# Query and key parts as three stored blocks, and the second-pass copies of the first two heads loaded behind the chunk loop

## What is computed

```python
xn = _layernorm(x, axis=-1)                      # x: 2048 tokens of 256
qkv = xn @ qkv_w.T + qkv_b
q, k, v = split(qkv)                             # 16 heads of width 16
scores = einsum('bqhd,bkhd->bhqk', q, k) / sqrt(16)
scores = where(causal, scores + slopes[h] * (pos_k - pos_q), -1e9)
attn = softmax(scores, axis=-1)
out = einsum('bhqk,bkhd->bqhd', attn, v) @ out_w.T + out_b
x = x + out * silu(experts(xn))                  # top 2 of 8 experts for each token
```

## Time and profile before

| what | value |
|---|---|
| runs | 852.41, 852.84, 845.97 us (median 852.41) |
| profiled execution | 851.59 us |
| its span, first to last instruction | 849.8 us |
| PE busy | 714.9 us (84%) |
| DVE busy | 584.8 us (69%) |
| ACT busy | 476.4 us (56%) |
| mean granted TensorE clock | 0.919 of full speed |

### The profile page before, as it was taken

One profiled execution on the slowest core, in us unless ns is written; L12 is line 12 of the kernel. 1 busy time (PEld: TensorE's weight loads), 2 busy tenths in 40 slices (PEclk: granted clock), 3 DMA queues, 4 the chain that ended last, 5 costly groups with the idle time before them and its releaser, 6 DMA issues.

```text
span 849.8 us, 14608 instructions
## 1 busy us (share of the span) xinstructions
PE 714.9 (84%) x5342; PEld 334.9 (39%) x5342; DVE 584.8 (69%) x1190; ACT 476.4 (56%) x990; POOL 156.3 (18%) x297
## 2 busy tenths in 40 slices
PE   3477788668889898998999999989999988888885
PEld 1244364333333444444344434434443442333433
DVE  5999776389667776777677667767776777974121
ACT  2277757450566566566656565656565566645551
POOL 1423250027600000000000100000000006720111
PEclk9688989785799999999999999999999999958998
DMA  9710223435470562253235325422522312330001
GB/s 295 253 35 7 87 90 116 120 96 164 154 134 5 148 127 82 76 128 87 70 105 131 94 72 122 130 70 81 123 87 70 110 70 70 113 118 1 26 26 50
DMA packets 76863, 83.76 MB, mean 99 GB/s; under 512 B 35485, under 2 KB 60512, under 8 KB 76448
## 3 DMA queue, kind: packets, MB, share of 16 engines
q1 hardware_dynamic: 70982, 71.96, 30.5%
q0 software_dynamic: 3280, 8.98, 3.4%
q10 hardware_dynamic: 2530, 1.89, 0.8%
HBM read 39.56 MB, written 25.43 MB: 76 GB/s over the span
## 4 chain that ended last, share of the span: by engine, by line
PE 55%; ACT 13%; DVE 9%; issue 7%; SPq 6%; DMA 4%; POOL 4%; ACTq 2%; POOLq 0%; DVEq 0%
PE bank L1535 15%; PE bank L1472 8%; ACT PR L805 7%; PE bank L1435 7%; PE bank L1445 5%; PE bank L1494 5%; PE bank L1550 4%; SPq L405 4%; PE bank L1307 3%; POOL XT L570 3%; DMA qk_parts<-TG 2%; DVE PM L1206 2%; PE bank L1350 2%; PE bank L1576 2%; ACT U L794 2%
## 5 line engine op out<-in xcount | busy, mean ns | idle before, releaser
L805 ACT ACTIVATE PR<-bank 128x512 f32<-128x512 f32 (+3 forms) x640 | 317.6, 537 | 254.4 <-PE bank L1494 145.3
L1206 DVE TENSOR_REDUCE PM<-bank 128x1 f32<-128x512 f32 (+3 forms) x640 | 354.7, 603 | 75.6 <-PE bank L1472 46.9
L1494 PE MATMUL bank<-OPS 57*128 57x512 f16 (+3 forms) x640 | 210.8, 366 | 54.3 <-ACT PR L805 47.6
L1472 PE MATMUL bank<-OPS 54*128 54x512 f16 (+3 forms) x640 | 197.0, 377 | 12.4 <-DVE PM L1206 8.3
L1535 PE MATMUL bank<-PR,VS 128*17 128x512 f32 (+3 forms) x1280 | 164.1, 565 | 0.0
L1494 PEld LDWEIGHTS bank<-OPS 57*128 57x128 f16 x640 | 53.0, 94 | 119.7 <-ACT PR L805 109.9
L1472 PEld LDWEIGHTS bank<-OPS 54*128 54x128 f16 x640 | 50.0, 95 | 120.3 <-DVE PM L1206 74.2
L538 POOL TENSOR_TENSOR NP<-NM,NIL 128x8 bf16<-128x8 f32 x32 | 7.7, 240 | 464.1 <-DVE NM L1214 463.9
L1435 PE MATMUL bank<-WB 128*128 128x256 f16 x552 | 80.8, 276 | 0.0
L1435 PEld LDWEIGHTS bank<-WB 128*128 128x128 f16 x552 | 46.4, 101 | 35.9 <-issue 29.4
L1504 PE MATMUL bank<-MASK 64*128 64x64 bf16 x512 | 59.6, 199 | 0.0
(11 more groups left out here) (179 smaller groups left out, 783.3 us busy)
## 6 DMA issues: line engine op xcount, KB each, us to landing
WB<-W SPq DMA_DIRECT2D x23, 512.0 KB, 3.8
OPS<-qk_parts SPq DMA_DIRECT2D x56, 128.0 KB
x_rows<-PR SPq DMA_DIRECT2D x23, 256.0 KB, 3.2
WB<-in_w SPq DMA_DIRECT2D x23, 256.0 KB, 3.5
y_rows<-XT SPq DMA_DIRECT2D x23, 256.0 KB, 3.1
OPS<-qk_parts SPq DMA_DIRECT2D x56, 64.0 KB
W<-in_w SPq DMA_DIRECT2D x6, 512.0 KB, 6.0
XT<-in_b SPq DMA_DIRECT2D x23, 128.0 KB, 4.0
```

Source lines behind the costliest of these rows:

```text
L805: act.activation(PR[:, tile % RING, off:CH], PS[2 + tile % 2][:, off:CH], ACT.Exp, scale=1 / SCORE).then_inc(b_exped, 1)
L1206: dve.tensor_reduce(PM[:, c % 2, j, xq, gg:gg + 1], bank[:, 0:width], AX.X, ALU.max).then_inc(a_reduced, 1)
L1472: last = mm(bank[:, 0:width], OPS[ROWS_A, slot, 0, P * (TC * a + xq):P * (TC * a + xq) + P], OPS[ROWS_A, slot, 1, CH * gg:CH * gg + width] ...
L1494: last = mm(bank[:, off:CH], OPS[ROWS_B, slot, 1, P * k:P * k + P], OPS[ROWS_B, slot, 0, CH * b + off:CH * b + CH], start=True, stop=k < T ...
```

## The change

The DRAM tensor qk_parts has three blocks a side instead of two, in the order in which OPS wants them: high, low, high for the queries, high, high, low for the keys. Each of the four staging buffers is therefore stored by two DMAs instead of one (STORES: first part, number of parts, block to write), 8 stores a chunk and 1.5 times the bytes. In return one load fills the 48 rows of one side of a row half (load_parts), and load(h) has 6 DMAs instead of 10.

The loads of heads 0 and 1 are divided. The position rows of row half 0 are loaded once, over all columns, ahead of the chunk loop (rows_in), behind three new waits for phi_q, scan_kv and numden, that the first layer is done with the memory of OPS. In the chunk loop only row half 0 is loaded, 4 loads a chunk. Row half 1 of both heads is loaded behind the loop and behind the UNITS loads, over all columns, with 6 loads (second_in), and the first tile of the second pass waits for it too. All counts of parts_out, first_in and opa_in follow.

```diff
--- before.py
+++ after.py
@@ -32,8 +32,8 @@
 POS = 6
 
 
-LOADS = (((0, 2, 1), (0, 1, 1)), ((0, 1, 2), (1, 1, 1)))
-HEAD_DMAS = 2 * (1 + len(LOADS[0]) + len(LOADS[1]))
+STORES = (((0, 2, 0), (0, 1, 2)), ((0, 1, 0), (0, 2, 1)))
+PART_DMAS = 2
 HALF_ROWS = P // 2
 ROWS = POS + 3 * HD
 ROWS_A = slice(0, ROWS)
@@ -240,7 +240,7 @@
         PROWS = [w2flat[0:ROWS8, 2 * WQG + 1024 * n:2 * WQG + 1024 * n + 1024].bitcast(F16) for n in range(2)]
 
 
-        parts = nc.dram_tensor("qk_parts", (2, 2, D, S), F16, kind="Internal").ap()
+        parts = nc.dram_tensor("qk_parts", (2, 3, D, S), F16, kind="Internal").ap()
         bias_rows = nc.dram_tensor("bias_rows", (3, 3 * D + E), BF16, kind="Internal").ap()
         all_rows = nc.dram_tensor("position_rows", (2, ROWS8, 2, S), F16, kind="Internal").ap()
         x_rows = nc.dram_tensor("x_rows", (SLOTS * BLOCKS, 2 * D), F16, kind="Internal").ap()
@@ -307,7 +307,7 @@
         parts_out = [sem(f"parts_out{m}") for m in range(4)]
         raw_in = [sem("raw_in0"), sem("raw_in1")]
         last_in = [sem("last_in0"), sem("last_in1")]
-        ones_in = sem("ones_in")
+        ones_in, rows_in, second_in = sem("ones_in"), sem("rows_in"), sem("second_in")
         mrow = [sem(f"mrow{s}") for s in range(NC)]
         x_in = [sem(f"x_in{c}") for c in range(NC)]
 
@@ -371,42 +371,32 @@
                 sp.wait_ge(x1_add, 2 * c + 2)
                 sp.dma_start(x1_dram[:, TC * c:TC * c + TC, :], XO[:, TC * c:TC * c + TC, :]).then_inc(x1_spill, 16)
 
+            def load_rows(h, half, done):
+
+                base = HALF_ROWS * half
+                sp.dma_start(OPS[base:base + POS, h % 4, :, :],
+                             all_rows[h // 8, POS * (h % 8):POS * (h % 8) + POS, :, :]).then_inc(done, 16)
+
+            def load_parts(h, half, cols, done):
+
+                base = HALF_ROWS * half
+                for side in range(2):
+                    sp.dma_start(OPS[base + POS:base + ROWS, h % 4, side, cols],
+                                 parts[side, :, HD * h:HD * h + HD, cols]).then_inc(done, 16)
+
             def load(h):
 
-                for base in (0, HALF_ROWS):
-                    sp.dma_start(OPS[base:base + POS, h % 4, :, :],
-                                 all_rows[h // 8, POS * (h % 8):POS * (h % 8) + POS, :, :]).then_inc(opa_in[h // 2 % 2], 16)
-                    for side in range(2):
-                        row = base + POS
-                        for first, parts_of, times_of in LOADS[side]:
-                            rows = HD * parts_of * times_of
-                            src = parts[side, first:first + parts_of, HD * h:HD * h + HD, :]
-                            if times_of > 1:
-                                src = src.broadcast_to([times_of, HD, S])
-                            sp.dma_start(OPS[row:row + rows, h % 4, side, :], src).then_inc(opa_in[h // 2 % 2], 16)
-                            row += rows
-
-            def first_load(c):
-
-                cols = slice(CH * c, CH * c + CH)
-                sp.wait_ge(parts_out[0], 16 * c + 16)
-                sp.wait_ge(parts_out[2], 16 * c + 16)
-                for base in (0, HALF_ROWS):
-                    for h in range(2):
-                        sp.dma_start(OPS[base:base + POS, h, :, cols],
-                                     all_rows[0, POS * h:POS * h + POS, :, cols]).then_inc(first_in[c], 16)
-                        for side in range(2):
-                            row = base + POS
-                            for first, parts_of, times_of in LOADS[side]:
-                                rows = HD * parts_of * times_of
-                                src = parts[side, first:first + parts_of, HD * h:HD * h + HD, cols]
-                                if times_of > 1:
-                                    src = src.broadcast_to([times_of, HD, CH])
-                                sp.dma_start(OPS[row:row + rows, h, side, cols], src).then_inc(first_in[c], 16)
-                                row += rows
+                for half in range(2):
+                    load_rows(h, half, opa_in[h // 2 % 2])
+                    load_parts(h, half, slice(0, S), opa_in[h // 2 % 2])
 
             sp.wait_ge(rows_kept[0], 32)
             sp.wait_ge(rows_kept[1], 32)
+            sp.wait_ge(phi_q, 2 * NC)
+            sp.wait_ge(scan_kv, 2 * NC)
+            sp.wait_ge(numden, 2 * NC)
+            for h in range(2):
+                load_rows(h, 0, rows_in)
             for c in range(NC):
                 cols = slice(CH * c, CH * c + CH)
                 if c + 2 < E // 2:
@@ -415,15 +405,22 @@
                 for m in range(4):
                     side, half = m // 2, m % 2
                     sp.wait_ge(qk_p1, 4 * c + m + 1)
-                    sp.dma_start(parts[side, :, half * P:half * P + P, cols].rearrange("j f t -> f j t"),
-                                 QP[m]).then_inc(parts_out[m], 16)
-                first_load(c)
+                    for first, parts_of, at in STORES[side]:
+                        sp.dma_start(parts[side, at:at + parts_of, half * P:half * P + P, cols].rearrange("j f t -> f j t"),
+                                     QP[m][:, first:first + parts_of, :]).then_inc(parts_out[m], 16)
+                sp.wait_ge(parts_out[0], 16 * PART_DMAS * (c + 1))
+                sp.wait_ge(parts_out[2], 16 * PART_DMAS * (c + 1))
+                for h in range(2):
+                    load_parts(h, 0, cols, first_in[c])
             sp.wait_ge(memset_done, 11)
             for h in range(4):
                 sp.dma_start(OPS[ROWS_MAX, h, 1, :].rearrange("j (q t) -> j q t", q=NT),
                              UNITS[:, :].unsqueeze(1).broadcast_to([3, NT, P])).then_inc(ones_in, 16)
+            for h in range(2):
+                load_rows(h, 1, second_in)
+                load_parts(h, 1, slice(0, S), second_in)
             for m in range(4):
-                sp.wait_ge(parts_out[m], 16 * NC)
+                sp.wait_ge(parts_out[m], 16 * PART_DMAS * NC)
             load(2)
             load(3)
 
@@ -732,7 +729,7 @@
                     values(c, range(TC))
                 for m in range(4):
                     act.wait_ge(qk_ps, 4 * c + m + 1)
-                    wait(act, parts_out[m], 16 * c)
+                    wait(act, parts_out[m], 16 * PART_DMAS * c)
                     if c == 0 and m == 0:
                         act.wait_ge(rows_kept[0], 32)
                         act.wait_ge(rows_kept[1], 32)
@@ -1460,9 +1457,10 @@
                 bank, slot, a, xq, gg = a_place(tile)
                 width = CH if gg < a else P * (xq + 1)
                 if p == 0 and tile == OFF[c]:
-                    pe.wait_ge(first_in[c], 16 * 2 * HEAD_DMAS)
+                    pe.wait_ge(rows_in, 16 * 2)
+                    pe.wait_ge(first_in[c], 16 * 2 * 2)
                 if tile % PER_PAIR == 0:
-                    wait(pe, opa_in[p % 2], 16 * 2 * HEAD_DMAS * ((p + 1) // 2))
+                    wait(pe, opa_in[p % 2], 16 * 2 * 2 * 3 * ((p + 1) // 2))
                 if tile < WIDE:
                     wait(pe, a_reduced, tile - 3)
                 else:
@@ -1491,6 +1489,7 @@
                     pe.wait_ge(mrow[c], 32 * (p + 1))
                     if tile == 0:
                         pe.wait_ge(ones_in, 16 * 4)
+                        pe.wait_ge(second_in, 16 * 2 * 3)
                 last = mm(bank[:, off:CH], OPS[ROWS_B, slot, 1, P * k:P * k + P],
                           OPS[ROWS_B, slot, 0, CH * b + off:CH * b + CH], start=True, stop=k < TC * b)
                 if k < TC * b:
```

## The result

| | kernel before | changed kernel |
|---|---|---|
| median, first comparison | 851.95 us (4 runs) | 841.7 us (837.14 to 845.22, 4 runs) |
| ratio, 95% interval | | 0.9878 (0.983 to 0.9925) |
| second comparison | 851.33 us (23 runs) | 844.17 us (6 runs), 0.9949 (0.9906 to 0.9992) |
| third comparison | 850.73 us (29 runs) | 843.33 us (12 runs), 0.9918 (0.9888 to 0.9947) |
| profiled execution's span | 849.8 us | 843.4 us |

The change is 7 to 8 us faster by the medians of the two later, larger comparisons; the ratio of the third, the largest, allows 4.5 to 9.5 us. The median of all 22 runs of the changed kernel is 843.6 us. The profile shows 6.4 us.

A forecast was written before the change was run, and what follows sets the result against it. SyncE's issue queue was taken to delay one expert fetch and, at its end, the UNITS loads. 851.6 - 8.0 (chunk stage) - 2.5 (last loads) = 841.1, against the median 841.9; forecast 841.5 us, range 839 to 844.5.

The forecast's parts named there:

- The row loads ahead of the loop: Waits and position-row loads ahead of the chunk loop: hidden in SyncE's 5.4 us wait, cost nothing; without that cover 0.7 us.
- The issue terms: SyncE's chunk loop: 0.45 us a store, 3.6 us for eight a chunk; four three-block loads 2.7 us instead of 12.5.
- the landing of chunk 3's stores: End of SyncE's chunk loop: 3.3 us, between 3.6 us of store issue and 2.7 us of loads, ending at 184.6.
- The chunk stage: Ahead of the score loop: earlier expert fetch and steady clock bring the first tile reduction from 188.93 to 180.9, 8.0 us.
- Without the 6.28 us gap I expect the granted clock to stay at 1.00 as in chunk 1: TensorE, chunk 2: no clock fall, so the last two value tiles come 2 x 0.65 us sooner.
- the stretch that I had named as a sign: Window 156 to 172 us: a granted clock of 1.00 there would show the forecast right.
- rival A: Chunks 0 and 1: four extra stores cost like full ones, 3.2 us instead of 1.3 each; 846.6 us, chance 0.18.
- The fetch: Second pair of expert fetches: issued at 143.4, landing 4.4 us later at 147.9, before ScalarE's own work ends at 150.0.
- The last loads: End of SyncE's list: second-pass loads land by 199, before TensorE wants them at 203.4; the UNITS wait goes, 2.5 us.
- rival C: Before the second pass: its loads become the new wait; landing at 208 gives 846; mild chance 0.08, slower 0.05.
- the queue let the last four go only by 229.26 ... some 18 us, 95 GB/s: Loads of heads 2 and 3 before: 1.73 MB in 18 us, so 0.86 MB of second-pass loads takes 9 us.
- Rival D: Second-pass tiles: without the 2.7 us stop the clock rises earlier, 3 to 6 us more gain, 836 us; chance 0.10.

The follow-up runs named there:

- the kernel with one-block loads: Changed kernel with its four second-pass loads of heads 0 and 1 cut into twelve one-block loads of 16 rows, same bytes: median 844.61 us, ratio 0.9929.

## Why the prediction was right, and where its sum was not

**The mechanism held.** The one fetch behind the loads was on the path: moving it alone moved the end of ScalarE's first parts of chunk 2 by 4.1 us, and the division of the loads alone by 5.6, about as much as the whole change (5.6 to 6.1). The row loads ahead of the loop cost nothing. The issue terms were close: a median of 0.47 and 0.49 us a store (queries and keys) instead of my 0.45, though the eight of chunk 0 took 5.5 us from first to last; 3.03 us for four loads where I had 2.7. For the landing of chunk 3's stores I had 3.3 us, a term that no row of mine shows; it took 1.15 us, but the stores began at 177.16 instead of 175, and the loop ended at 185.17 instead of 184.6.

**The chunk stage, 8.0 us foretold, 5.8 measured (6.1 from the spill).** The step that failed is "Without the 6.28 us gap I expect the granted clock to stay at 1.00 as in chunk 1", and it failed twice. First in 146 to 154 us, ahead of the stretch that I had named as a sign: TensorE began the projections of chunk 2 at 149.24 (149.3 foretold), but they took 6.80 us instead of 5.34 (7.00 and 6.82 in the other two profiles), so their last bank came near 156.0 instead of 154.7, and ScalarE's first parts ended at 157.0 instead of 155.5. In the first profile the last thing that ScalarE waited for there was a store that landed at 156.25, which looks like rival A. But in the other two it waited for TensorE and ended hardly earlier (47.3 and 47.6 us from the spill, against 47.8), so the stores as such are worth at most 0.5 us here. What larger stores may cost is TensorE's longer pause in front of these matmuls, 2.1 to 2.3 us in every kernel with three blocks; that the pause brought the clock down is likely and not shown. The fetch was mis-sized too, 7.1 us from issue to the cast (143.80 to 150.91) and not the 4.4 of before, but it was not what ended last.

The second fall was 0.57 in 162 to 166 us, where six matmuls took 1.50 us again, and the cast at 170.99 came at 165.16 instead of 163. This one is a matter of luck: of the kernels identical up to there, one profile stayed at 1.00, two had 0.57 in one window, and the kernel with one-block loads had 0.50 from 162 to 176, with 25.2, 25.9 to 26.2 and 29.5 us to the first reduction. So this term is not a number but a spread, and a range should have held it.

**The last loads, 2.5 us foretold, 0.7 measured.** Here rival C came true in its mild form: its mechanism and its landing (208), not its price (846), since the first pass was later as well and TensorE waited only 2.06 us. I had them land by 199; they landed at 206.85. The step that failed: "the queue let the last four go only by 229.26 ... some 18 us, 95 GB/s". I took the moment at which the queue issues the last load as the moment at which the data has landed, and so read 1.73 MB in 18 us from rows that show only when it was issued. Measured, 0.86 MB took 17.8 us from the issue at 189.07 to 206.85, 48 GB/s. Nobody waited for the loads of heads 2 and 3 in the kernel before, so no row held their landing, and the bound should have been open upward.

The rule of the Trainium skill ("DMA: Bandwidth & Descriptors", section "Why a DMA increments its semaphore by 16 and not by 1"), that a transfer is spread over as many engines as divide the outermost size of both sides, I had cited and then let give the same 9 us as my row. Both changes of form that it allows for (16 rows, and 48 rows as one run) took the wait away, so these runs agree with it; which engines were busy no run showed. By it four loads of 64 KB an engine over three engines, at the 27 GiB/s that the same page states for an engine in its section "Specifications", would be an estimate of 9 us; the measured 17.8 us is twice that, and the measurement decides.

**The total.** 7 to 8 us by the later medians, 6.4 by the profiles. 841.5 met the first median of four runs within 0.2 us, and that is luck: the sum was 10.5 us and the profiled difference 6.4. Against the later medians it is 2 to 3 us low, by the terms above. Rival D did not show in the first profile: in windows of 10, 10, 20 and 20 us from the first second-pass matmul on the clock was 0.67, 0.84, 0.91 and 1.00 in both kernels.

## What to carry to other kernels

When an engine's queue is full of issues, look in the list for the one item that somebody waits for. Moving it gave here two thirds of what thinning the list gave, and then the next item behind the same pile was wanted; ask for that one before choosing. Loads put at the end of a list must be costed to their landing, from a row in which somebody waited for such a load; the row of the issue gives only a lower bound. And lay blocks that one load gathers out as one run: the same bytes and the same number of loads then kept the DMA engines busy for 96% of the time instead of 43%. To compare kernels whose clocks differ, find a position ahead of the clock's swing and a stretch of equal work behind it, and read the two apart.

## What the runs showed of the hardware

The form of a transfer set its time more than its size: 0.86 MB as 3 x 16 rows a load landed 14.3 us after the last issue, the same bytes as 16 rows a load within 9.1. While such loads were under way the DMA engines were busy for 43% of the time with the first form, and for 96% with one run of 48 rows. Its issue changes too: 0.77 us for two loads of 48 rows in one run, 1.50 for two of 3 x 16.

The score loop took one of two times for a pair of heads, 76.7 us or 77.8 to 78.0 us, in the first five full pairs of all thirteen profiles. The table of windows of the changed kernel, a pair a row:

```profile
296.31:373.00 76.69, 70.26 (x615) 33.25 (x614) 54.96 (x113) 45.95 (x104) 4.90 (x22) 1.00 0.38 101
373.00:449.69 76.69, 70.26 (x615) 33.27 (x614) 54.96 (x113) 45.95 (x104) 4.90 (x22) 1.00 0.41 98
449.69:527.62 77.93, 71.52 (x615) 33.38 (x614) 55.05 (x113) 45.96 (x104) 4.90 (x22) 0.98 0.39 100
527.62:605.50 77.88, 71.48 (x615) 33.53 (x614) 55.05 (x113) 45.97 (x104) 4.90 (x22) 0.98 0.37 98
605.50:682.17 76.67, 70.26 (x615) 33.27 (x614) 54.95 (x112) 45.95 (x104) 4.89 (x22) 1.00 0.29 91
```

Work and order are the same; a pair at a granted clock of 0.98 takes 1.2 us more than one at 1.00. Which pairs are hit differs from execution to execution. The stage ahead of the loop has its own spread: for the same work from ScalarE's first parts of chunk 2 to the first reduction 25.2 us at 1.00, 29.5 us at 0.50. Up to 3.8 us between the six pairs of one kernel and up to 4.3 us there can make up much of the 10 us between single runs, and so a gain of 2 us was plain in the positions and not in the medians.
